# A two-layer transformer stack on one Trainium2 core: attention's maxima taken four places later, and block ends without GpSimd's drain

## The reference, cut to what matters

```python
x = x + jnp.tanh(g_xattn[0]) * _L0_xattn_ref(_layernorm(x, axis=-1), ctx_512, ctx_512)
x = x + jnp.tanh(g_ffn[0]) * _L0_ffn_ref(_layernorm(x, axis=-1), ...)   # 8 experts, top 2, and a shared one
x = x + jnp.tanh(g_xattn[1]) * _L1_xattn_ref(_layernorm(x, axis=-1), ctx_512, ctx_512)
x = x + jnp.tanh(g_ffn[1]) * _L1_ffn_ref(_layernorm(x, axis=-1), ...)   # 32 experts, top 6, and a shared one

# attention, the same in both layers: 32 query heads of 16, 8 key/value heads, 4 query heads to each
scores = jnp.einsum('bkgsd,bktd->bkgst', qh, kh) / sqrt(16)
attn = jax.nn.softmax(scores, axis=-1)
out = jnp.einsum('bkgst,bktd->bkgsd', attn, vh)
```

## Time and profile before

| | |
|---|---|
| median of three runs | 2057.18 us |
| the profiled execution's own time | 2056.58 us |
| its span, first to last instruction | 2054.9 us |
| mean granted TensorE clock | 0.966 of full speed |
| TensorE, VectorE, ScalarE, GpSimd busy | 92%, 66%, 56%, 38% |
| attention of layer 0 | from 2.4 to 427.3 us |
| experts of layer 0 | to 936.8 us |
| barrier between layers | to 937.9 us |
| attention of layer 1 | to 1361.8 us |
| experts of layer 1 | to 2054.9 us |

### The profile page before, as it was taken

The page is one execution under the profiler, slowest core; times in us unless marked ns, Lnnn a source line. Parts: engine busy times, 40 slices in busy tenths (PEclk is TensorE's granted clock), DMA queues, the critical chain, the costliest instruction groups (busy, mean ns, idle before and its releaser), DMA issues. The chain is left out here.

```text
span 2054.9 us, 40817 instructions
## 1 busy us (share of the span) xinstructions
PE 1884.4 (92%) x10024; PEld 1220.0 (59%) x10025; DVE 1348.5 (66%) x2556; ACT 1144.9 (56%) x1856; POOL 783.2 (38%) x941
## 2 busy tenths in 40 slices
PE   4999999989999999993999999977888999999998
PEld 2333333344888877881433333344667888888886
DVE  6899988841445444434989898848995555555553
ACT  1777777743322335541677777762224666666664
POOL 3222222125301125553222222136653665565655
PEclk9999999989999999995899999988999999999998
DMA  4422222143111358765422222222026889899986
GB/s 139 119 59 65 59 66 69 35 146 120 52 52 62 134 171 197 144 110 138 120 61 67 62 61 63 52 87 87 1 73 178 197 188 207 201 201 203 199 197 107
DMA packets 100083, 233.53 MB, mean 114 GB/s; under 512 B 17410, under 2 KB 20484, under 8 KB 99972
## 3 DMA queue, kind: packets, MB, share of 16 engines
q1 hardware_dynamic: 61572, 137.75, 23.6%
q0 software_dynamic: 33792, 79.71, 20.1%
q10 hardware_dynamic: 4608, 14.68, 2.1%
HBM read 127.23 MB, written 57.67 MB: 90 GB/s over the span
## 5 line engine op out<-in xcount | busy, mean ns | idle before, releaser
L599 DVE TENSOR_REDUCE maxima<-ring_ps 128x1 f32<-128x512 f32 x1024 | 639.6, 680 | 89.3 <-PE ring_ps L386 88.5
L493 ACT ACTIVATE probs<-score_ps 128x1024 f32<-128x1024 f32 x512 | 501.7, 1018 | 91.6 <-PE score_ps L403 89.3
L386 PE MATMUL ring_ps<-k_turned,q_turned 64*128 64x512 f32 x1024 | 414.5, 482 | 39.3 <-DMA q_turned<-q_lo 18.4
L386 PEld LDWEIGHTS ring_ps<-k_turned,q_turned 64*128 64x128 f32 x1024 | 178.9, 193 | 366.7 <-DVE maxima L599 256.9
L1179 PE MATMUL bank_f<-w_gu_parts_f,xg_T_f 128*128 x1800 | 367.3, 352 | 2.6 <-issue 2.6
L1179 PEld LDWEIGHTS bank_f<-w_gu_parts_f,xg_T_f 128*128 128x128 f32 x1800 | 325.6, 190 | 30.8 <-issue 3.3
L403 PE MATMUL score_ps<-q_turned,k_turned 64*128 64x512 f32 x1024 | 336.7, 447 | 1.7 <-ACT probs L493 1.2
L420 PE MATMUL out_ps<-probs,v_ones 128*32 128x512 f32 x2048 | 273.3, 606 | 11.0 <-issue 10.3
L1204 PE MATMUL bank_f<-w_dn_parts_f,hg_T_f 96*128 (+1 forms) x888 | 242.9, 409 | 2.1 <-DVE hg_T_f L1771 1.5
L984 POOL DMA_INDIRECT xg_f<-xh_rows_f,idx_in_f x156 | 160.2, 1027 | 183.5 <-DVE idx_in_f L1661 116.8
L1000 POOL DMA_INDIRECT out_x<-y_tok_f,idx_out_f x111 | 176.8, 1593 | 131.5 <-ACT y_tok_f L1405 94.7
(11 more groups left out here) (231 smaller groups left out, 2343.4 us busy)
## 6 DMA issues: line engine op xcount, KB each, us to landing
w_gu_f<-in_L_w_gu SPq DMA_DIRECT2D x64, 384.0 KB
q_turned<-q_hi SPq DMA_DIRECT2D x128, 128.0 KB, 2.6
w_raw_f<-in_L_w_sh_gu ACTq DMA_DIRECT2D x28, 512.0 KB, 3.5
w_dn_f<-in_L_w_dn SPq DMA_DIRECT2D x32, 384.0 KB
k_turned<-k_hi SPq DMA_DIRECT2D x128, 64.0 KB, 2.1
q_turned<-no_max SPq DMA_DIRECT2D x64, 128.0 KB, 2.6
q_turned<-q_lo SPq DMA_DIRECT2D x64, 128.0 KB, 2.6
w_gu_f<-in_L_w_gu SPq DMA_DIRECT2D x16, 512.0 KB
```

Source lines behind the costliest of these rows:

```text
L386: pe.matmul(ring(k, "max", i), q_turned[rows, slot, h // 2, c * P:(c + 1) * P], k_turned[rows, slot, :], start=True, stop=True).then_inc(m ...
L493: act.activation(probs[:, (TPB * u + c) % PROBS, pair, :, :], score_ps[:, pair, :, :], ACT.Exp, scale=float(D) ** -0.5).then_inc(exped, 1)
L599: dve.tensor_reduce(maxima[:, par, col:col + 1], ring(k, "max", i), AX.X, ALU.max).then_inc(max_taken, 1)
```

## The change

`AHEAD` goes from 4 to 0. Now all 16 places of step k hold the tiles of unit k − 1, tile by tile. Nothing else in the attention is written otherwise; the waits that count maxima follow from `max_place`. Step 0 then has no first scores, and step 32, which had 12, has 16.

The blocks of attention and experts are made with `no_gpsimd_drain=True`. The small block in front of all, which makes the identity matrix, stays as it was. The barrier between the layers is among four engines, without GpSimd, and the semaphores are cleared in it; SP then increments a new semaphore, and GpSimd waits for that.

```diff
@@ -27,7 +27,7 @@
 PLACES = 7
-AHEAD = 4
+AHEAD = 0
@@ -142,7 +142,7 @@
-        block = ctx.enter_context(nc.Block())
+        block = ctx.enter_context(nc.Block(no_gpsimd_drain=True))
@@ -1843,6 +1843,7 @@
+        cleared = ctx.enter_context(nc.semaphore("cleared"))
@@ -1882,7 +1883,9 @@
-        nc.all_engine_barrier(sems_to_clear=range(min(numbers), max(numbers) + 1))
+        nc.multi_engine_barrier([e.engine for e in (nc.sync, nc.scalar, nc.vector, nc.tensor)], sems_to_clear=range(min(numbers), max(numbers) + 1))
+        nc.sync.nop().then_inc(cleared, 1)
+        nc.gpsimd.wait_ge(cleared, 1)
```

## The result

The changed kernel took 2049.02 us (median of 7 runs, 2047.49 to 2049.87) against 2057.18 (7 runs, 2054.8 to 2060.15); the ratio is 0.996, with a 95% interval of 0.9949 to 0.9971, that is 6.0 to 10.5 us less. The forecast was 2051.4, in a range of 2048.3 to 2056. The direction and the two main terms were right; some 2.5 us of the gain, in the full steps, were not in the sum.

What follows compares the result with a forecast made beforehand. TensorE was taken to bound a full step, not the stage's two ends. 4.8 − 2.6 + 3.1 + 0.2 = 5.5 us off the profiled 2056.58 (2051.1) or the median 2057.18 (2051.7) gave 2051.4, range 2048.3 to 2056.

Steps and rivals of the forecast that it cites:

- the full steps: Attention's steps between its two ends: bound by TensorE, no instruction added, nothing moves, price 0.
- The fill: Start of each attention stage: everything hung on step places comes four maxima sooner, 2.4 us gained a layer, 4.8 in all.
- The tail: Last steps of each attention stage: four maxima move into step 32, costing 1.3 us a layer, bounds 0.7 to 2.4.
- full steps get shorter: Rival on attention's full steps: later placements and fewer semaphore waits save 0.1 us in 62 steps, total 2045; chance 0.06.
- The split's slack: GpSimd's split of the maxima, before TensorE asks at line 356: 2.3 us to spare in even steps.
- The clock: TensorE's clock rise in the fill: taken as 0; 0.6 us a layer lost if it doesn't move with earlier work.
- The joint: From layer 0's experts to layer 1: 3.1 us gained without GpSimd's drain, bounds 2.8 to 3.3; the barrier itself 0.
- the drain's time isn't given back: Rival at the block ends: GpSimd's leftover work or the landing turns up elsewhere, 3.1 and 0.2 us go, 2054.7; chance 0.13.
- the 2.8 end of the bounds: Joint's lower gain: if GpSimd is really busy until 936.6 and its first memset waits, 0.3 us come back.
- The program's end: End of the program: leaving out GpSimd's drain gains 0.2 us, since SP was ready at 2054.4.
- Attention's ends: Ends of the attention blocks: no gain, since GpSimd's drain is over before VectorE, which waits for x, arrives.

Runs made afterwards that it cites:

- −3: The changed kernel with AHEAD = -3, VectorE's wait on max_split at place 0 and the last steps' statistics behind place 2: 2065.5 us.
- −2: The changed kernel with AHEAD = -2 and the last steps' statistics behind place 1: 2049.23 us; with VectorE's wait on max_split at place 0 too, 2047.07 us.

## Why the prediction was right, and where it wasn't

**The fill** was forecast at 2.4 us a layer and measured at 2.38 (turn of q) to 2.48 (first exponential score). Right, as was its reason: all of it hangs on places in a step.

**The tail** was forecast at 1.3 us a layer, measured at 0.98 in both (9.26 to 10.24); from the last transpose to the experts' first row it is 19.3 us before and 19.4 after. It lies within the bounds given. Why it is less than in the full even step that it was read from was not looked into.

**The full steps** were set at 0, and that is the step that failed. "So no instruction is added to a full step" was true and not enough: one wait changed its place. It gave 1.28 us in layer 0. In layer 1 the difference is 0.95, the step of the clock's rise having been 0.6 longer. With that step left out of the 30, six stages with AHEAD = 4 took 342.0 to 342.3 us and ten with AHEAD = 0 and VectorE's wait at place 0 alone took 340.7 to 341.2: 1.2 us a layer between the means, 2.5 in all, some 30% of the whole. The rival *full steps get shorter* said 0.1 us a step for fewer waits, with a chance of 0.06; its size per step was near and its total of 6 us over twice too large, since 12 of 30 steps gained nothing; its cause was beside the point, for the number of waits is the same. The argument against it ("a step is bound by matmuls whose number stays") took the step as bound by one engine. Inside it TensorE's scores of places 5, 11 and 15 (14 in odd steps) follow VectorE's reductions of places 2, 8 and 12 by 0.05 us, so that what delays one of these three delays the step. That 2049.0 still lay in the range is owed to the range's width, which was worked out from other terms.

**The split's slack** was read rightly from the earlier trace rows: 2.3 us, no new waits at line 356. After, an even step's split ends at 380.57 and TensorE takes it at 382.89. At the 0.6 us a place of the expectation for −3, 0.5 us of it would be left there. It was gone: −2 hardly waits (3.9 us in 12 waits), −3 in nearly every step, since VectorE idles for 0.28 us ahead of place 0 and for 0.30 ahead of place 2 and reduces them later than back to back.

**The clock.** The step in which the rise falls took 13.82 and 13.81 us after; over the profiles with AHEAD = 4 and the wait in its old place it was 13.20 to 13.83, mean 13.54; with AHEAD = 0 13.10 to 13.84, mean 13.66. A rise that stays behind by 2.4 us would, by the forecast's own price, have shown as 0.6 more; the means differ by 0.1, with a scatter of 0.7. The rise itself can be read from the granted clock of layer 1: with AHEAD = 4 and the wait in its old place it went from 0.50 to 1.00 at 31.3, 32.0 and 34.4 us behind the first score, with AHEAD = 0 at 28.7 to 32.0, mean 30.3. Behind the first transpose of maxima it came at 14.3, 15.0 and 17.4 us, and with AHEAD = 0 at 14.1 to 17.4, mean 15.7: the same mean distance from the work. 0 agrees with that; the scatter of 3 us is larger than the shift of 2.4, so that these profiles speak for a rise that moves along and don't prove it.

By the Trainium skill (TensorE: Matmul & The Clock Gate, section What's actually happening) the clock follows recent activity; the means agree with a rise that moves along with the work.

**The joint** was forecast at 3.1 and measured at 3.4 us, of which 0.4 are an earlier landing. Over all profiles the old joint took 9.3 to 9.6 us and the new one 6.0 to 6.5, 3.2 between the means. SP was through 4.8 us after the last scatter's start (5.2 before), the barrier took 1.1 to 1.2 us in both. GpSimd was not busy behind the barrier: its first memset came with SP's nop. So the rival *the drain's time isn't given back* is out. Its "for", that GpSimd still does something then, was wrong: the time goes with the drain, as the run with the old barrier showed.

The Trainium skill (PSUM — Partial Sum Buffer, section Engine vs sequencer instructions) says that a drain waits for the engine to go idle. That gave the 2.8 end of the bounds; the drain of 6.442 us that began after all transfers had landed shows that here it cost as much with no transfer left to wait for and no instruction of GpSimd's running in the profile.

**The program's end** was forecast at 0.2 and gave 0 (5.15 us in both). **Attention's ends**: 0, as forecast.

The terms as measured in the two profiles: −4.8 (fill) + 2.0 (tail) − 2.2 (steps) − 3.4 (joint) = −8.4 us. With −0.5 ahead of the first scores, +0.1 behind the last transposes and +0.9 in the experts' stages, none of which is the change's as far as the profiles show, that is the −7.9 of the span. The times show 8.2 (6.0 to 10.5).

What stays open: what GpSimd does in its drain, and why it ends 6.4 to 7.0 us behind GpSimd's last operation in layer 0's experts and 3.3 to 3.6 behind it in layer 1's. Why 12 of the 30 steps don't gain was not traced either. Why AHEAD = −4 makes some steps 13.4 us long was not looked into.

## What to carry to other kernels

When work is moved inside a software pipeline, follow the waits that move with it, also those that never wait. Here a fulfilled wait beside the wait for another engine made the reduction start 0.07 us later behind that engine, and an idle VectorE didn't hide it. It lengthened the step at the three places whose reduction TensorE's later score follows at once, and was free at the place with 0.7 us to spare. So put such a wait where the result is not wanted at once. A drain of GpSimd after DMAs of its own is to be left out everywhere between two stages or nowhere: whichever barrier still has it pays it, and pays more when it starts late. In this kernel SP's wait for the landing of the scatters stands in its place.

## What was not expected of the hardware

GpSimd's drain took 6.442 us when it started behind the landing of all its DMAs, and 8.202 us when it was started with the last scatter: the time is not that of the landing. Where the drain was called behind the last operation it ended 6.4 to 7.0 us after that operation (before: 928.31 + 1.56 = 929.87 to 936.6, 6.7). A second, fulfilled wait ahead of a reduction put an instruction of 21 ns between TensorE's score and the reduction, which started 0.11 us behind the score and not 0.04.
